# Expert routing in a decoder: mirrored compares in the merges of a sort, a last merge stopped at blocks of 64, and ranks of group sums found by halving

## The reference, cut to what matters

```python
scores = softmax(x @ Wr + br)                          # (T, 64)
order = jnp.argsort(-scores, axis=0)                   # every expert sorts all tokens
sorted_vals = jnp.take_along_axis(scores, order, axis=0)
group_score = sorted_vals.reshape(T // 64, 64, 64).sum(axis=1)   # 32 groups of 64 tokens per expert
_, top_flat = jax.lax.top_k(group_score.reshape(-1), 32 * 16)    # 512 best of 2048 groups
# all tokens of a chosen group keep their score, the others get 0
fs = jnp.where(mask, scores, 0.0)
return fs / (fs.sum(axis=-1, keepdims=True) + 1e-06)
```

## Time and profile before

| | |
|---|---|
| device time, median of 3 runs | 5069.64 us |
| the three runs | 5078.28, 5069.64, 5061.39 us |
| span of the profiled execution | 5066.8 us |
| profiled execution's own time | not listed apart from its span |
| busy in the span | PE 81%, DVE 69%, ACT 49%, POOL 27% |
| mean granted TensorE clock | 0.883 of full speed |

### The profile page before, as it was taken

How to read it: one execution, slowest core, us unless ns; L and a number is a source line. 1 busy time by engine, 2 the same in 40 slices (tenths; PEclk the granted TensorE clock), 3 DMA queues, 4 the chain that set the end, 5 groups by cost and what they waited for, 6 DMA issues and landing times. The chain is left out here.

```text
span 5066.8 us, 77700 instructions
## 1 busy us (share of the span) xinstructions
PE 4085.0 (81%) x29323; PEld 2224.5 (44%) x29323; DVE 3485.7 (69%) x5453; ACT 2507.2 (49%) x3544; POOL 1378.9 (27%) x1033
## 2 busy tenths in 40 slices
PE   5640696999999999999995995866996767888883
PEld 3630234666666666666652332432443332222232
DVE  5579444777777777777784445766773558888868
ACT  2120243666666666666662223543564344677772
POOL 0000300566666666666664303000000100000000
PEclk5565798999999999999997996987997687999996
DMA  0010001000000000000003106316650333323300
GB/s 19 1 60 0 0 0 51 1 14 1 14 1 14 14 1 14 1 14 1 1 1 130 58 0 150 53 15 102 84 77 4 90 59 62 55 48 53 49 3 9
DMA packets 135603, 167.70 MB, mean 33 GB/s; under 512 B 19498, under 2 KB 108092, under 8 KB 134676
## 3 DMA queue, kind: packets, MB, share of 16 engines
q1 hardware_dynamic: 127540, 146.39, 14.3%
q0 software_dynamic: 6528, 16.42, 1.3%
q10 hardware_dynamic: 1184, 0.12, 0.0%
HBM read 125.31 MB, written 34.55 MB: 32 GB/s over the span
## 5 line engine op out<-in xcount | busy, mean ns | idle before, releaser
L3001 POOL TENSOR_TENSOR arena<-arena 128x512 f32<-128x512 f32 (+1 forms) x768 | 1131.7, 1475 | 692.0 <-ACT arena L2957 638.6
L2452 ACT ACTIVATE arena<-ps 128x1024 f32<-128x1024 f32 (+1 forms) x688 | 703.3, 1023 | 333.7 <-PE ps L2377 323.0
L2470 DVE TENSOR_REDUCE arena<-ps 128x2 f32<-128x826 f32 (+1 forms) x576 | 564.9, 981 | 185.3 <-PE ps L2323 177.5
L3017 DVE TENSOR_TENSOR arena<-arena 128x1024 f32<-128x1024 f32 (+1 forms) x448 | 644.9, 1478 | 13.8 <-ACT arena L2984 13.8
L3039 DVE TENSOR_TENSOR arena<-ps,arena 128x512 f32<-128x512 f32 (+1 forms) x768 | 530.4, 691 | 178.5 <-ACT arena L2951 144.4
L2323 PE MATMUL ps<-arena 48*128 48x413 bf16 (+3 forms) x1920 | 436.4, 334 | 135.9 <-DVE arena L2470 67.2
L2951 ACT ACTIVATE arena<-ps 128x1024 f32<-128x1024 f32 (+1 forms) x448 | 410.3, 960 | 205.1 <-PE ps L2879 197.0
L2863 PE MATMUL ps<-arena 128*128 128x256 f32 (+1 forms) x1664 | 444.0, 392 | 20.5 <-DVE arena L3025 19.2
L2957 ACT ACTIVATE arena<-arena 128x1024 f32<-128x1024 f32 (+1 forms) x448 | 425.0, 992 | 50.7 <-DVE arena L3017 48.2
L2396 PE MATMUL ps<-arena 128*9 128x256 f32 (+2 forms) x5504 | 436.2, 389 | 10.5 <-ACT arena L2440 7.7
L2879 PE MATMUL ps<-arena 64*128 64x256 f32 (+1 forms) x3328 | 427.3, 391 | 5.5 <-ACT arena L2973 1.3
(11 more groups left out here) (647 smaller groups left out, 5810.8 us busy)
## 6 DMA issues: line engine op xcount, KB each, us to landing
arena<-ctx_parts SPq DMA_DIRECT2D x96, 200.1 KB
arena<-ctx_parts SPq DMA_DIRECT2D x192, 100.1 KB
arena<-in_ctx_feat SPq DMA_DIRECT2D x8, 1601.0 KB, 6.4
arena<-in_ctx SPq DMA_DIRECT2D x16, 768.0 KB
arena<-diff_att_stack SPq DMA_DIRECT2D x60, 192.0 KB
ctx_parts<-arena SPq DMA_DIRECT2D x24, 400.2 KB, 3.8
arena<-in_w SPq DMA_DIRECT2D x1, 6416.0 KB, 18.3
arena<-in_ctx_feat SPq DMA_DIRECT2D x8, 800.5 KB
```

Source lines behind the costliest of these rows:

```text
L2452: act.activation(self.prob[0:rows, u % 3, :], self.ps[0:rows, 2 * (u % 2):2 * (u % 2) + 2, :].rearrange("p n c -> p (n c)"), ACT.Exp).then ...
L2470: ins = dve.tensor_reduce(dst[:, :, j // 2], self.ps[:, 4:6, 0:hi - lo], AX.X, ALU.max)
L3001: pool.tensor_tensor(acc[0:rows, u % 2, :], before, sc[0:rows, u % 2, t, :], ALU.add).then_inc(added, 1)
L3017: dve.tensor_tensor(e, e, mb[0:rows, u % 2, None, :].to_broadcast([rows, n, 2 * S]), ALU.subtract).then_inc(sub_done, 1)
```

## The change

The merges below length 1024 no longer make blocks in alternating order. Every block is sorted falling, and a merge of two falling blocks begins with a compare in which the second block is read backwards (`mirrored`, an access with step -1), followed by plain compares of halving distance. All 55 compares are now two instructions of 512 elements; nine of them (k from 4 to 1024) are mirrored. The last merge, behind the exchange across partitions, stops at distance 64: four compares in place of ten. Each block of 64 then holds the right elements in no particular order, the group sums are taken over these, and a new reduction `low` takes the smallest element of each block. The memset of `e["fs"]` is moved from its place behind L1188 to a place ahead of the wait for the matmul of `diag`. In place of sixteen ranks there are five (sizes 16, 8, 4, 2, 1): each counts the sums above one probe of a partition, and by that count a half of the partition's sums is kept for the next. The probes and their counts go to `small[:, 7]` and `small[:, 0]`.

```diff
-        above = [st.sb(f"above{k}", [P, NG * P]) for k in range(2)]
+        above = st.sb("above", [P, NG * P])
+        low = st.sb("low", [P, NG])
...
-            def compare(k, j, both):
+            def compare(j, mirrored):
...
-                for up in range(2 if both else 1):
-                    if both:
-                        v = lambda t, side: t[:, :].rearrange("p (g u n s j) -> p g u n s j", u=2, s=2, j=j,
-                                                              n=k // (2 * j))[:, :, up, :, side, :]
-                    else:
-                        v = lambda t, side: t[:, :].rearrange("p (n s j) -> p n s j", s=2, j=j)[:, :, side, :]
-                    tt(v(b, 0), v(a, 0), v(a, 1), ALU.min if up else ALU.max)
-                    ins = tt(v(b, 1), v(a, 0), v(a, 1), ALU.max if up else ALU.min)
-                link(ins)
+                v = lambda t, side: t[:, :].rearrange("p (n s j) -> p n s j", s=2, j=j)[:, :, side, :]
+                other = lambda side: v(a, side)[:, :, ::-1] if mirrored else v(a, side)
+                tt(v(b, 0), v(a, 0), other(1), ALU.max)
+                link(tt(v(b, 1), v(a, 1), other(0), ALU.min))
                 cur = 1 - cur
 
             k = 2
             while k <= HALF:
-                j = k // 2
+                compare(k // 2, k > 2)
+                j = k // 4
                 while j >= 1:
-                    compare(k, j, k < HALF)
+                    compare(j, False)
                     j //= 2
                 k *= 2
...
-            while j >= 1:
-                compare(HALF, j, False)
+            while j >= GR:
+                compare(j, False)
                 j //= 2
-            ranked = buf[cur]
-
-            link(dve.tensor_reduce(gs[:, :], ranked[:, :].rearrange("p (g r) -> p g r", r=GR), AX.X, ALU.add))
+            ranked = buf[cur][:, :].rearrange("p (g r) -> p g r", r=GR)
+
+            link(dve.tensor_reduce(gs[:, :], ranked, AX.X, ALU.add))
             tt(diag[:, :, :], ident[:, None, :].to_broadcast([P, NG, P]), gs[:, :, None].to_broadcast([P, NG, P]),
                ALU.mult).then_inc(s["diag_ready"], 1)
+            dve.tensor_reduce(low[:, :], ranked, AX.X, ALU.min)
+            dve.memset(e["fs"][:, :], 1.0)
             dve.wait_ge(s["spread_ready"], 1)
-            for g in range(NG):
-                if g >= 2:
-                    dve.wait_ge(s["dve_own"], link.n - 1)
-                link.n += 1
-                ts(above[g % 2][:, :], ps[:, 0:4, :].rearrange("p n c -> p (n c)"), gs[:, g:g + 1], 0.0,
-                   ALU.is_gt, ALU.add, accum_out=small[:, 0, g:g + 1]).then_inc(s["dve_own"], 1)
-            dve.wait_ge(s["dve_own"], link.n)
-
-            link(ts(small[:, 4, :], small[:, 0, :], float(BUDGET), -BIG, ALU.is_ge, ALU.mult))
-            link(tt(small[:, 4, :], small[:, 4, :], gs[:, :], ALU.subtract))
-            link(dve.tensor_reduce(cols[:, 0:1], small[:, 4, :], AX.X, ALU.max))
+            part, size, r = gs[:, :], NG, 0
+            while size >= 1:
+                half = size // 2
+                at = max(half - 1, 0)
+                probe = part[:, at:at + 1]
+                link(ts(above[:, :], ps[:, 0:4, :].rearrange("p n c -> p (n c)"), probe, 0.0, ALU.is_gt, ALU.add,
+                        accum_out=small[:, 0, r:r + 1]))
+                dve.tensor_copy(small[:, 7, r:r + 1], probe)
+                if half:
+                    link(ts(cols[:, 7:8], small[:, 0, r:r + 1], float(BUDGET), -BIG, ALU.is_lt, ALU.mult))
+                    nxt = small[:, 6 - r % 2, 0:half]
+                    link(stt(out=nxt, in0=part[:, 0:half], scalar=cols[:, 7:8], in1=part[:, half:size], op0=ALU.add,
+                             op1=ALU.max))
+                    part = nxt
+                size, r = half, r + 1
+
+            link(ts(small[:, 4, 0:r], small[:, 0, 0:r], float(BUDGET), -BIG, ALU.is_ge, ALU.mult))
+            link(tt(small[:, 4, 0:r], small[:, 4, 0:r], small[:, 7, 0:r], ALU.subtract))
+            link(dve.tensor_reduce(cols[:, 0:1], small[:, 4, 0:r], AX.X, ALU.max))
...
-            low = ranked[:, :].rearrange("p (g r) -> p g r", r=GR)[:, :, GR - 1]
-            link(tt(small[:, 7, :], small[:, 6, :], low, ALU.max))
+            link(tt(small[:, 7, :], small[:, 6, :], low[:, :], ALU.max))
...
-            link(dve.memset(e["fs"][:, :], 1.0))
```

## The result

The changed kernel takes 5014.45 us, the median of four executions (5005.38 to 5020.49), against 5068.27 for the kernel before (four executions, 5061.39 to 5078.28): a ratio of 0.9896, with a 95% interval of 0.9877 to 0.9914. The profiled execution was the slowest of the four (5020.49 us, span 5018.7), 48.1 us under the span of before.

The account below looks back on a forecast made before the run. The prediction took the routing to be bound by a chain of VectorE instructions; 6.9 (sort) + 8.0 (last merge) + 22.2 (ranks) + 2.2 (memset) = 39.3 us off the median 5069.6 gave 5030.3 us, range 5019 to 5045.

Parts of the forecast that it names:

- The chain: Routing, 359.7 to 534.3 us: a chain of VectorE instructions, so each us taken off it comes off the kernel.
- The sort, 6.9 us: Sort of the halves: 45 compares become two instructions of 512 each, 66.74 us to 59.85, backward reads taken as free.
- rival (a): Mirrored compares of sort and merge: backward reads pay, giving back 6.5 us (5037) or 13 us (5043); chance 0.18.
- the price that the prediction drew from the Trainium skill: Backward-read compares: by section 5.2's letter 1.73 instead of 1.054 ns per column, making the sum 6.2 us smaller.
- The last merge, 8.0 us: Merge behind the exchange: six compares, distances 32 to 1, go at 1.33 us each.
- The ranks, 22.2 us: Rank passes: sixteen become five linked rounds of 2.96 us, the last shorter, 36.47 us to 14.3; the largest term.
- The bounds written beside the sum: Rank rounds: 13.6 us if the small instructions cost 0.17 each, 14.8 us if each costs 0.27, around 14.3.
- The memset, 2.2 us: Memset leaves the chain behind L1188; with `low`, 3.5 us hidden in VectorE's 5.4 us matmul wait, 1.9 us cover left.
- The sum, 39.3 us: Whole kernel: 6.9 + 8.0 + 22.2 + 2.2 us gained, taken off the median of 5069.6.
- rival (b): Start of expert MLPs: gain given back behind the barrier by a later clock rise, 5055 to 5085 us; chance 0.05.
- the MLPs start in the same state, only earlier: Expert MLPs: argument against (b), since the last 20 us ahead of the barrier, mask and 32 small matmuls, are the same.
- The range: Whole kernel's median: 5019 to 5045 us, to hold 8 in 10, including part of the backward-read rival.

## Why the prediction was wrong, point by point

- *The chain.* Right: what was taken off VectorE between 359.7 and 534.5 us came off the time.
- *The sort, 6.9 us.* 80.0 us up to the exchange became 73.06: 7.0. The backward reads cost 0, as taken, and rival (a) is out. Out, too, is the price that the prediction drew from the Trainium skill, Vector Engine (DVE) Microarchitecture Reference, section 5.2: neither a step of -1 nor a step of two words slows a two-tensor instruction here (0.69 us in both cases). "In rising order" was my reading of it; the page says nothing of order there, and its 1.73 ns is for a source that hops 4 KiB at every element. The remark that negative steps were not measured stands in its section 5.1, not in 5.2.
- *The last merge, 8.0 us.* 13.30 became 5.31: 8.0.
- *The ranks, 22.2 us.* 36.47 became 14.07: 22.4. A round is 2.90 us from pass to pass, I had 2.96; the instruction of one element takes 0.18 and not 0.21. The bounds written beside the sum do not follow from its terms: with 0.17 or 0.27 us for each of the eight small ones they are 13.8 and 14.6, not 13.6 and 14.8.
- *The memset, 2.2 us.* 3.56 us from L1188 to the scan became 1.31: 2.25. Its cover held, but the wait for the matmul did not keep its length: it ends 0.7 us later (9.68 instead of 8.95 for the stretch), so that 2.87 us of it are left and not 1.9. The eight matmuls took 6.04 us instead of 5.32, at a clock of 0.57 instead of 0.62. This is the one term inside the routing that I had called free of a reason to change.
- *The sum, 39.3 us.* The routing gave 38.9.
- *What failed* is the step against rival (b): "the MLPs start in the same state, only earlier". They start in nearly the same state (0.4 us of the surplus lie between the reciprocal and their first activation: 21.6 us before, 21.2 after), but earlier is not neutral. The two falls of the clock in the 190 us behind the routing, one of which stood in the earlier trace rows, were a property of when its gaps came. With the change both are gone, 7.0 us less (190.6 to 183.6). I had rival (b) only as a loss. The mechanism stood in the prediction, with one of its two signs left out.
- The difference up to 3000 us is thereby accounted for: 38.9 us of the routing, 0.4 ahead of the MLPs and 7.0 in them are 46.3, of which 1.7 are given back in the stages up to there, and 44.6 are left. Why the falls come at one place in time and not at another was not tried.
- *The range* failed by a second step, the larger one in microseconds: I put its centre on the median of three executions and allowed the new median after as much as those three strayed. The executions of one kernel have a standard deviation of 7 to 8 us and span up to 38. The measured 5014.45 lies 15.9 us under the forecast of 5030.3: 6.4 because the median of three, 5069.64, lay that much above the mean of 60 executions, 5.0 from the surplus above, and 4.5 because four executions of the changed kernel were low. Against its mean of ten, 5018.9, the range of 5019 to 5045 would have missed by a hair. That the miss came out as large as it did was the draw, which the one pair of profiles puts behind 3000 us.

## What to carry to other kernels

When a stage is shortened, look in the stage behind it for stretches below full clock that border on a short gap of TensorE: each of them may vanish or appear with the new start, and each is worth half of its length (3.3 us for 7 here), with either sign. Put the range of a forecast on the scatter of the executions as well as on the terms; three executions understate it. A surplus or a shortfall is best placed by adding the saved time back as a plain delay: if it goes, it was the timing and not the code. And where late stages scatter, compare the profiles at one instruction ahead of them: here that gave the 5 us to a few tenths, for which the whole times needed dozens of executions.

## What the runs showed of the hardware

- A gap of 1.7 us of TensorE after some 45 us of nearly full work was followed by about 7 us at 1.2 GHz in some kernels (2.07 us for a pair of matmul records) and by none in others (1.12 us), and which of the two held was the same in both profiles of the kernel before and in both of the changed kernel. Each such fall cost 3.3 us. A delay of 0.8, 1.7 or 2.5 us ahead gave one, two and no falls, in one profile each.
- Two executions of one kernel kept in step to 0.2 us, falls of the clock included, from the start of the sort up to 3000 us (2686.25 and 2686.43 us, and twice 2641.65), and then parted: by 9.8 us at the end in the changed kernel.
- An operand of 512 f32 read at step -1 costs the same 0.69 us as one read forward, beside a second tensor operand, and so does a compare that takes every second word.
